# Moving the B and C projections of a state-space layer behind the x transposes, and signalling its second state matrix in two halves

## What is computed

```
zxbcdt = x_normed @ W_in.T                 # z 1024, x 1024, B 64, C 64, dt 16 columns
dt     = softplus(dt + dt_bias)
xBC    = silu(conv4(xBC) + conv_b)         # causal convolution over 4 tokens, per column
h      = h * exp(dt*A) + dt * B_t x_t      # 16 heads, 64 x 64 state, 192 steps
y_t    = h C_t;   y = (y + D*x) * silu(z)
out    = (y * rsqrt(mean(y*y) + eps) * norm_w) @ W_out.T
```

## Time and profile before

| | |
|---|---|
| median of 3 runs | 1842.42 us (1842.16 to 1848.24) |
| profiled execution | 1848.1 us, of which the span from first to last instruction is 1846.4 us |
| mean granted TensorE clock over the span | 0.906 |
| PE busy | 1606.8 us (87%) |
| DVE, POOL, ACT busy | 953.4, 777.2, 682.7 us (52%, 42%, 37%) |
| the layer | about from 413 to 1147 us of the span: PE busy 600.9, DVE 526.1, ACT 383.4, POOL 356.4 us, granted clock 0.83 |

### The profile page before, as it was taken

One profiled execution on the slowest core, in us unless ns is written; L12 is line 12 of the kernel. 1 busy time (PEld: TensorE's weight loads), 2 busy tenths in 40 slices (PEclk: granted clock), 3 DMA queues, 4 the chain that ended last, 5 costly groups with the idle time before them and its releaser, 6 DMA issues. The chain is left out here.

```text
span 1846.4 us, 29417 instructions
## 1 busy us (share of the span) xinstructions
PE 1606.8 (87%) x8779; PEld 1128.2 (61%) x8780; DVE 953.4 (52%) x2196; ACT 682.7 (37%) x1471; POOL 777.2 (42%) x638
## 2 busy tenths in 40 slices
PE   7999999985799989988989761089999999999996
PEld 7999999954557657574747431055555555555553
DVE  5554545425578986877778554133333333333332
ACT  2525252506487583745547210022222222222221
POOL 4220200011224264757464657545455554545454
PEclk9999999987799997979889675589999999999998
DMA  7110000015244344333413110177777776776665
GB/s 271 61 58 1 12 1 12 2 58 197 78 109 147 91 120 117 89 100 89 143 40 99 36 22 15 30 197 175 157 157 181 157 173 160 163 180 166 157 114 92
DMA packets 96680, 195.20 MB, mean 106 GB/s; under 512 B 38392, under 2 KB 46880, under 8 KB 91857
## 3 DMA queue, kind: packets, MB, share of 16 engines
q0 software_dynamic: 36992, 88.26, 22.2%
q1 hardware_dynamic: 59600, 105.78, 19.3%
HBM read 144.15 MB, written 49.84 MB: 105 GB/s over the span
## 5 line engine op out<-in xcount | busy, mean ns | idle before, releaser
L1868 PE MATMUL moe_ps_gu<-moe_wgu,moe_xt 128*128 x960 | 333.2, 490 | 0.0
L1742 POOL DMA_INDIRECT out_h<-moe_yy,moe_idx_s x121 | 190.9, 1578 | 274.9 <-DVE moe_idx_s L1797 138.1
L1015 POOL DMA_INDIRECT scratch_slots<-lay_toki,lay_slot x192 | 215.9, 1124 | 59.0 <-issue 58.2
L1868 PEld LDWEIGHTS moe_ps_gu<-moe_wgu,moe_xt 128*128 128x128 f32 x960 | 173.7, 191 | 98.0 <-issue 1.7
L1852 PE MATMUL moe_ps_y<-moe_wd,moe_ht 96*128 x484 | 228.8, 595 | 3.4 <-DVE moe_ht L1823 3.1
L1780 ACT ACTIVATE moe_sl<-moe_ps_gu 128x192 f32<-128x192 f32 x120 | 39.7, 331 | 443.7 <-PE moe_ps_gu L1868 318.4
L1196 PE MATMUL lay_ring<-lay_xnt,win_sb 128*128 128x128 f32 (+2 forms) x1152 | 173.2, 299 | 23.4 <-ACT lay_xnt L1096 18.1
L1196 PEld LDWEIGHTS lay_ring<-lay_xnt,win_sb 128*128 128x128 f32 (+2 forms) x1152 | 155.2, 203 | 32.9 <-ACT lay_xnt L1096 18.8
L1412 DVE SCALAR_TENSOR_TENSOR lay_xa<-lay_ring,head_cw,lay_xa 128x378 f32<-128x378 f32 (+5 forms) x240 | 142.4, 609 | 58.6 <-ACT lay_xa L1067 52.6
L1280 PE MATMUL lay_ring<-head_wout,lay_yb 128*128 128x512 f32 x384 | 171.3, 600 | 0.0
L1736 POOL DMA_INDIRECT moe_xg<-scratch_xg,moe_idx_g x123 | 131.1, 1066 | 47.4 <-issue 22.1
(11 more groups left out here) (284 smaller groups left out, 2744.9 us busy)
## 6 DMA issues: line engine op xcount, KB each, us to landing
lay_m<-scratch_cum SPq DMA_DIRECT2D x16, 1536.0 KB
moe_wgu<-in_wgu SPq DMA_DIRECT2D x32, 768.0 KB
moe_wd<-in_wd SPq DMA_DIRECT2D x32, 384.0 KB
out_h<-lay_hres SPq DMA_DIRECT2D x48, 128.0 KB
scratch_xg<-lay_x SPq DMA_DIRECT2D x48, 128.0 KB
win_sb<-in_win SPq DMA_DIRECT2D x1, 4384.0 KB, 15.9
tok_u_raw<-in_tok_u SPq DMA_DIRECT2D x16, 256.0 KB, 4.0
tok_v_raw<-in_tok_v SPq DMA_DIRECT2D x16, 256.0 KB, 4.9
```

The lines of the kernel that those rows point to most:

```text
L1015: pool.indirect_dma_start(out=a["slots"], out_offset=bass.IndirectOffsetOnAxis(ap=slot[:, j, k:k + 1], axis=0), in_=toki[:, j:j + 1], in_o ...
L1742: pool.indirect_dma_start(out=a["out"], out_offset=bass.IndirectOffsetOnAxis(ap=idx_s[n][:, 0:1], axis=0), in_=yy[n][:], in_offset=None, b ...
L1868: last = mm(ps_gu[b][:], xt[b][:, t], wgu[:, bass.ds(r * KD + t, 1)].rearrange("p o n -> p (o n)"), start=t == 0, stop=t == KD - 1)
```

## The change

Four things change, all in the layer. (1) TensorE makes the B and the C projection of pair n+1 together behind the six x transposes of pair n (`project_bc`); before, B stood ahead of the transposes and C behind them, at the head of the next iteration. `ring_order()` follows. (2) VectorE convolves B and C one after the other behind all six `x_dt`, the reciprocal's product (`routed_shift`) and, in the last pairs, the router's steps, and ahead of `state_matrix(n, 1)`; before, B was convolved between the third and fourth `x_dt` and C behind the state matrix. (3) ScalarE takes both first taps ahead of the Exp of `dtn`, which now has a wait of its own for the Abs, and ahead of the routed rows. (4) `state_matrix(n, 1)` is two instructions of eight heads, each with a signal; TensorE waits for the first ahead of y4 and for the second ahead of y6.

```diff
@@ def ring_order():
-    order = [("bc", 0, 0)]
+    order = [("bc", 0, 0), ("bc", 0, 1)]
     for i in range(-1, PAIRS + 1):
         n = i + 1
-        if n < PAIRS:
-            order.append(("bc", n, 1))
...
-        if n + 1 < PAIRS:
-            order.append(("bc", n + 1, 0))
         if n < PAIRS:
             order += [("xt", n, k) for k in range(N_XT)]
+        if n + 1 < PAIRS:
+            order += [("bc", n + 1, 0), ("bc", n + 1, 1)]
@@ scalar
-                def steps_in(i):
+                def projected_bc(i):
                     src = halves("bc", i, 0)[NS:NS + NH]
                     nc.scalar.activation(dtr[:], src, ACT.Identity, bias=dtb[:]).then_inc(dtr_done, 1)
-                    own.step(nc.scalar.activation(dtn[:], src, ACT.Abs, bias=dtb[:]))
+                    size = own.mark(nc.scalar.activation(dtn[:], src, ACT.Abs, bias=dtb[:]))
+                    first_tap(i, "bc", 0, TB)
+                    first_tap(i, "bc", 1, TC)
+                    own.wait(size)
                     own.step(nc.scalar.activation(dtn[:], dtn[:], ACT.Exp, scale=-1.0))
@@ tensor
-                def project_b(i):
+                def project_bc(i):
                     pe.wait_ge(xnt_done, i + 1)
-                    project(i, "bc", 0, *BC_TILES[0][:2])
+                    for k in range(2):
+                        project(i, "bc", k, *BC_TILES[k][:2])
...
-                    if pairs(n):
-                        project(n, "bc", 1, *BC_TILES[1][:2])
                     if pairs(i):
-                        pe.wait_ge(m_done, i * 2 + 1)
+                        pe.wait_ge(m_done, i * 3 + 1)
                         pe.wait_ge(xdt_done, i * N_XT + N_XT)
                         for m2 in range(4):
                             state_products(i, 0, m2)
-                    if pairs(i):
-                        pe.wait_ge(m_done, i * 2 + 2)
                     for m2 in range(4):
                         if pairs(i):
+                            pe.wait_ge(m_done, i * 3 + 2 + m2 // 2)
                             state_products(i, 1, m2)
...
-                    if pairs(n + 1):
-                        project_b(n + 1)
                     if pairs(n):
                         for k in range(N_XT):
                             x_transposes(n, k)
+                    if pairs(n + 1):
+                        project_bc(n + 1)
@@ vector, state_matrix(i, b)
-                    v.scalar_tensor_tensor(m0[:, b], m0[:, b], 1.0, gm[:, b].unsqueeze(1).to_broadcast([P, NH, SEQ]),
-                                           ALU.min, ALU.mult).then_inc(m_done, 1)
+                    for h0, h1 in ((0, NH),) if b == 0 else ((0, NH // 2), (NH // 2, NH)):
+                        v.scalar_tensor_tensor(m0[:, b, h0:h1], m0[:, b, h0:h1], 1.0,
+                                               gm[:, b].unsqueeze(1).to_broadcast([P, h1 - h0, SEQ]),
+                                               ALU.min, ALU.mult).then_inc(m_done, 1)
@@ vector, the loop
                 conv(0, 0)
+                conv(0, 1)
                 for i in range(-1, PAIRS + 1):
-                    if pairs(n):
-                        conv(n, 1)
...
                     for k in range(N_XT):
                         if pairs(n):
                             x_dt(n, k)
-                        if k == 2 and pairs(n + 1):
-                            conv(n + 1, 0)
...
+                    if pairs(n + 1):
+                        conv(n + 1, 0)
+                        conv(n + 1, 1)
                     if pairs(n):
                         state_matrix(n, 1)
```

More of the change, by code:

```diff
@@ L1117, in _ @@
                 rows_in(0)
-                steps_in(0)
-                first_tap(0, "bc", 0, TB)
+                projected_bc(0)
                 for i in range(-1, PAIRS + 1):
@@ L1122, in _ @@
                     if pairs(n):
-                        first_tap(n, "bc", 1, TC)
                         steps_out(n)
@@ L1162, in _ @@
                     if pairs(n + 1):
-                        steps_in(n + 1)
-                        first_tap(n + 1, "bc", 0, TB)
+                        projected_bc(n + 1)
                     if pairs(i):
@@ L1307, in x_transposes @@
                     last.then_inc(ring_pe, 1)
-                def project_b(i):
+                def project_bc(i):
                     pe.wait_ge(xnt_done, i + 1)
-                    project(i, "bc", 0, *BC_TILES[0][:2])
+                    for k in range(2):
+                        project(i, "bc", k, *BC_TILES[k][:2])
                 token_rows(0)
-                project_b(0)
+                project_bc(0)
                 for i in range(-1, PAIRS + 1):
                     n, r, w = i + 1, i - 1, i - 2
-                    if pairs(n):
-                        project(n, "bc", 1, *BC_TILES[1][:2])
                     if pairs(i):
-                        pe.wait_ge(m_done, i * 2 + 1)
+                        pe.wait_ge(m_done, i * 3 + 1)
                         pe.wait_ge(xdt_done, i * N_XT + N_XT)
```

## The result

The changed kernel takes 1783.75 us (median of 4 runs, 1780.1 to 1790.4) beside 1842.3 us for the kernel before on the same chip: a ratio of 0.967, with a 95% interval of 0.963 to 0.971. The profiled execution took 1780.1 us (span 1778.3, mean granted clock 0.928 for 0.906).

A forecast was written before the change was run, and what follows sets the result against it. TensorE was taken as the bound, with its pause and late-read signals (the hold) as losses. Pairs 0 to 2 and four list pairs gave 4 + 3 + 0 + 4 x 9 = 43 us: 1800 us, range 1787 to 1837.

The forecast's parts named there:

- The pause: TensorE's 2.88 us wait ahead of the fifth transposed x tile; without it and its half clock y0 begins 3.9 us earlier.
- Pair 2: VectorE bounds this stretch and its work has not shrunk: gain nothing, range 3 down to -0.5 us.
- pairs 0 and 1: Pairs of sequences in the layer, without the large term: gains of 4 and 3 us.
- the four list pairs: Pairs 3 to 6, where GpSimd gives out lists: gain of 9 us each.
- the hold: Behind the y tiles TensorE's signals are read 1.6, 5.9 and 8 us late, until near GpSimd's last list's end.
- The period of about 76 us: Sign expected in pairs 3 to 6 of the layer: about 76 us a pair, for 85.
- the price of the hold: Gain in pairs 3 to 6 from escaping late signals, bounded by GpSimd's lists and gates: 9.9 us, taken as 9.
- the outer bound: Most that pairs 3 to 6 could gain each: 12 us, from 791 to 803, were the gates no bound.
- the tiles end behind the lists: Reason for the lower bound in pairs 3 to 6: tiles end behind the lists wherever they begin, gain nothing.
- rival 3: TensorE stands in short pieces in the hold, then runs the projections at half clock, net 14 us a pair: 1855; chance 0.07.
- Rival 4: y4 waits for the half matrix, or the sixth transposed tile for its x_dt, over 2.9 us: 1842; chance 0.05.
- Rivals 1 and 2: In list pairs the hold pays nothing (1835, chance 0.14), or pays in part, 3 to 6 us (1819, chance 0.12).

The follow-up runs named there:

- e13: State matrix halves alone on the kernel before, on a chip without the hold: 1785.1 us, ratio 1.000 to the kernel before.
- e1: Changed kernel with its second state matrix in one piece again, on a chip without the hold: 1812.2 us, ratio 1.016 to the kernel before.
- e17: State matrix halves alone on the kernel before, on a chip with the hold: 1841.1 us, ratio 0.998 to the kernel before.
- e10: Changed order with the second state matrix in one piece, on a chip with the hold: 1815.1 us, ratio 0.983 to the kernel before.
- e6: The kernel before, unchanged, run again for its trace on a chip with the hold: 1846.7 us, ratio 1.000.
- e9: The kernel before with eighteen lists behind rstd instead of fourteen, on a chip with the hold: 1874.8 us, ratio 1.018.
- e16: The changed kernel again, on another chip with the hold: 1801.8 us, ratio 0.976 to the kernel before.

## Why the prediction was wrong in size

**Right, step by step.** The pause and its half clock are gone in pairs 0 to 6, y0 stands 6.0 us behind o2 (5.8 forecast), the halves take 1.7 us each, the skips begin 13.5 us behind o2 (13.3), y4 begins about 1 us behind the first half's end (0.5 forecast), R0's copy 0.7 us behind R0 (under 3). Pair 2 gives -0.1 (nothing); pairs 0 and 1 give 6.5 and 4.4 (4 and 3). Most of the gain lies in the four list pairs, and the hold ends with the lists and carries it. The period of about 76 us was too long: 72.4.

**The step that failed** is the price of the hold: "GpSimd bounds the gain: lists to 788.7, two gate_y of 3.43 us to 795.6", 9.9 us a pair, of which I took 9, with 12 as the outer bound. Measured: 13.0 in pair 4 by the period, and 13.3 on average by the start of z. I had let the end of the gates move z one for one. The gates ended 32.4 us behind o2, even later than the 31.3 that this step gives them, and yet z began at 24.1, for 38.7 before. By the program's semaphores the gates bind only the sixth z tile, by way of ScalarE's silu and its bank, so z may begin five tiles ahead of their end: it began 8.2 us ahead, where before it was 2.5. The outer bound failed by its other half, that "the tiles end behind the lists". In my working R1 is read near 786 and R2 at 790.3, and z stands no earlier than 791, 26.7 us behind o2. The hold began 6 us later than I had it and caught only R2 and y7, by 2 and 4 us, so the last logits came before the last list's end and z with them.

What bounds a pair once the hold is short is VectorE: e13 has a period of 71.7 us in the old order without any hold, so 13.7 us were to be had in pair 4, and 13.0 came. Of the 3.9 us that VectorE still stood idle in pair 4 of after (waits above 0.15 us), 3.1 were for the late y7. GpSimd has its share in that floor by another way: `mk` in e13 and the two additions in after stand some 4 us each beside the gates, on an engine that has next to no idle time. With 13.3 for 9 the sum is 60 and the forecast 1782. A smaller slip: by its own price of 14 us for 14 tiles, rival 3 turns slower from about 13 tiles at half clock and not from 11, two being slow already.

**What only the repeats showed.** The gain differs: 58.5, 38.6, 58.1 and 46.6 us in the four sets of runs with the hold. The forecast's 43 lies among them, and a hit there would have been luck: a list pair gives 13 us where TensorE keeps its clock behind the gaps at y2, and some 7 where it doesn't (85.4 to 79 and 78), and the forecast has neither. That is rival 3's mechanism at another place: not the short pieces behind R0 but a gap within the y tiles, and at a price of 6 us, not 14. The change was faster in all four. Rival 4 was the one guarded against by the halves: in e1 TensorE waited 1.55 us for the state matrix, and there, without the hold, the kernel was slower than before. Rivals 1 and 2 are out for pairs 3 to 6: R0's copy came 10.5 us ahead of the last list's end.

**The lock.** By the rule of the Trainium skill (SBUF — State Buffer, Who interferes with whom), an exclusive lock on the port pair that VectorE and GpSimd share, a list could get through between the two halves, as I used it. In pairs 3 to 6 of after none did: in pair 4 one took 4.66 us across both. In pair 7 of the same kernel one did (2.38 us, then 1.36 for the next), and in the old order too (e17), where the last list came some 1.4 us sooner. When the list is issued does not decide it: in pair 6 it begins 0.20 us behind the first half's start and is kept out, in pair 7 it begins 0.21 us behind it and gets through. What does decide it is not shown.

**Open.** Why the hold begins 14 us behind o2 in the old order and 20 in the new. That it is the order's doing and not the halves' is shown by e10 and e17, but the order takes away TensorE's pause as well, and no run parts the two where the hold shows. Whether TensorE's signals come late or its work itself: in the hold its instructions stand in small groups, with idle times of 0.2 to 1.1 us put down to nothing (782.99 to 788.70 in pair 4 of before), and the ends of its matmuls are modelled. Why some chips have it at all; the five groups ran on five chips and none came twice, so that it stays with a chip is not shown either, and whether the first result's chip is one of them is not known. Why TensorE keeps its clock behind some gaps at y2 and not behind others. What the changed kernel takes on a chip without the hold.

## What to carry to other kernels

Before an engine is taken as the bound of a gain, name the instruction on the critical path that waits for it, and count what may run ahead of that instruction: here the gates bound the sixth z tile, and I had moved the first with them. The floor is the engine with no idle time left. A wait that the profile puts down to nothing it knows may belong to the chip and not to the program: time the same kernel on a second chip before pricing it, and a change on several before quoting its gain. When a tile is moved ahead of the work that feeds it, signal that work in the pieces in which it is used: here a wait of 1.55 us was followed by 20 us at half clock, and the kernel took 1812 us for 1785.

## What was new about the hardware

- The same kernel takes 1842 to 1848 us in four sets of runs and 1785 in two, the five groups being on five chips. In the four, readers of TensorE's tiles come up to 10 us late in this kernel (R0's copy, e6) while GpSimd gives out its last lists (14 us with eighteen lists in a row, e9); in the two they come within 0.7 us at full clock, with lists of the same 0.98 us.
- Idle times of well under 1 us within the y tiles can be followed by a long stretch at half clock, and need not be: 0.65 and 0.24 us at y2 by 23.9 us at 0.55 (e16), 0.65 and 0.20 us at the same place by 15.8 us at 1.00 (after, pair 3). 1.55 us at y4 were followed by 20.4 us at 0.50 (e1).
- One VectorE instruction of 0.21 us took 4.20 us as GpSimd's last list and gate ran beside it (e13), and the ranks' tile on TensorE began right behind it. In pair 4 of after it was two small additions that took 3.90 us beside the gates, for 0.97 in before.
